# First-layer products of the coupling network made once, and its stages put in one rolling order over all cycles

## The reference

```python
def _twist(x):
    o_r, o_i, p_r, p_i = jnp.split(x, 4, axis=-1)
    return jnp.concatenate([p_r, -p_i, -o_r, o_i], axis=-1)
gf = _global_net(x.mean(axis=1, keepdims=True), ...)
out = x
for _ in range(NUM_CYCLES):                        # 3
    tf = _coupling_net(out, ...)   # gelu(h @ w1 + b1), 256 to 256; gelu to 128; gelu to 64; sigmoid to 1
    combined = 0.7 * gf + 0.3 * tf
    coupling = 0.1 + adaptive_range * (combined - 0.5) * 2.0
    out = out + coupling * _twist(out)
```

## Time and profile before

| what | value |
|---|---|
| median of 3 runs | 1000.38 us (997.75 to 1003.14) |
| profiled execution, its own time | 1000.18 us |
| its span in the trace | 998.4 us |
| PE busy | 925.4 us, 93% |
| DVE, ACT, POOL busy | 563.0, 473.3, 372.3 us |
| last piece of the attention's output product ends, coupling stages begin on PE | 886.28 us |
| last matmul | ends at 985.9 us |

### The profile page before, as it was taken

The page is one execution under the profiler, slowest core; times in us unless marked ns, Lnnn a source line. Parts: engine busy times, 40 slices in busy tenths (PEclk is TensorE's granted clock), DMA queues, the critical chain, the costliest instruction groups (busy, mean ns, idle before and its releaser), DMA issues.

```text
span 998.4 us, 20489 instructions
## 1 busy us (share of the span) xinstructions
PE 925.4 (93%) x6821; PEld 839.2 (84%) x6822; DVE 563.0 (56%) x1308; ACT 473.3 (47%) x1459; POOL 372.3 (37%) x498
## 2 busy tenths in 40 slices
PE   5999999999999897999999973899999999998994
PEld 3589999999999675999999973799999999985662
DVE  7564545555555483434433445777777776663273
ACT  0255555555555233443444452655555655534442
POOL 5153343343333203122222225756656543324132
PEclk9899999999999979999999995999999999999997
DMA  9400000020000065677777731200000000000002
GB/s 274 143 1 2 1 0 1 2 64 2 1 0 1 1 212 218 241 251 244 246 258 262 242 94 45 56 12 23 11 21 16 17 2 1 2 1 1 1 1 84
DMA packets 37503, 76.15 MB, mean 76 GB/s; under 512 B 5101, under 2 KB 23777, under 8 KB 37313
## 3 DMA queue, kind: packets, MB, share of 16 engines
q1 hardware_dynamic: 34033, 66.03, 20.0%
q0 software_dynamic: 3408, 9.31, 2.9%
HBM read 66.02 MB, written 9.31 MB: 75 GB/s over the span
## 4 chain that ended last, share of the span: by engine, by line
PE 85%; DVE 7%; POOL 2%; DMA 2%; ACT 2%; issue 2%; POOLq 0%; DVEq 0%; SPq 0%; ACTq 0%
PE banks L1527 14%; PE banks L470 11%; PE banks L472 11%; PE banks L471 11%; PE banks L504 9%; PE banks L478 7%; PE banks L489 6%; PE banks L496 3%; PE banks L619 3%; PE banks L1754 2%; PE banks L375 1%; PE banks L1758 1%; POOL W L1213 1%; DVE region_a L2060 1%; PE banks L1762 1%
## 5 line engine op out<-in xcount | busy, mean ns | idle before, releaser
L1527 PE MATMUL banks<-region_b,region_a 128*128 128x128 f32 x1248 | 145.9, 275 | 1.2 <-DMA region_a<-in_L_ffn_W 0.7
L1527 PEld LDWEIGHTS banks<-region_b,region_a 128*128 128x128 f32 x1248 | 142.8, 192 | 1.7 <-issue 0.9
L1090 ACT ACTIVATE region_a<-banks,negmax 128x154 f32<-128x154 f32 x256 | 96.0, 389 | 90.9 <-DVE negmax L833 89.6
L1243 POOL TENSOR_TENSOR region_a<-region_a,recip 128x512 f32<-128x512 f32 x64 | 66.5, 1040 | 178.6 <-DVE recip L839 178.6
L1278 POOL TENSOR_TENSOR region_a<-region_a,recip 128x640 f32<-128x640 f32 x64 | 80.2, 1253 | 104.0 <-DVE recip L965 103.7
L1617 DVE SCALAR_TENSOR_TENSOR region_b<-banks,region_a,region_b 128x128 f32<-128x128 f32 x156 | 43.9, 344 | 109.7 <-PE banks L1527 109.0
L504 PE MATMUL banks<-region_a 128*128 128x128 f32 x768 | 96.6, 276 | 1.9 <-DVE oT_low L856 1.8
L504 PEld LDWEIGHTS banks<-region_a 128*128 128x128 f32 x768 | 91.0, 192 | 2.9 <-issue 2.2
L478 PE MATMUL banks<-region_a 128*128 128x308 f32 x256 | 77.1, 424 | 0.0
L470 PE MATMUL banks<-Wo_high,oT_high 128*128 128x256 f32 x256 | 75.8, 296 | 0.9 <-DVE oT_low L856 0.9
L1152 ACT CAST pT_high<-banks 128x640 fp32r<-128x640 f32 x64 | 44.4, 694 | 66.3 <-PE banks L619 66.3
(11 more groups left out here) (248 smaller groups left out, 2454.0 us busy)
## 6 DMA issues: line engine op xcount, KB each, us to landing
region_a<-in_L_ffn_W SPq DMA_DIRECT2D x39, 1024.0 KB, 4.9
y_slots<-region_b SPq DMA_DIRECT2D x39, 128.0 KB
W<-in_L_ffn_W SPq DMA_DIRECT2D x1, 4096.0 KB, 17.3
xn_rows<-region_b SPq DMA_DIRECT2D x1, 2048.0 KB, 8.4
out<-x SPq DMA_DIRECT2D x4, 512.0 KB, 2.9
x<-in_x SPq DMA_DIRECT2D x1, 1536.0 KB, 13.0
region_b<-in_L_xattn_Wq SPq DMA_DIRECT2D x1, 1024.0 KB, 11.3
region_b<-in_L_xattn_Wo SPq DMA_DIRECT2D x1, 1024.0 KB, 13.9
```

The costliest lines, as they stand in the source:

```text
L1090: e = act.activation(pr[:, j, 0:L.keys], scores[:, g % 2, u, i * L.keys:(i + 1) * L.keys], ACT.Exp, bias=negmax[:, g % 2, j:j + 1], accum_ ...
L1243: pool.tensor_tensor(whole, pr[:, :, 0:split], rc.broadcast_to([P, L.hs, split]), ALU.mult)
L1527: mm = pe.matmul(banks[:, 2 * r + part, m * P:(m + 1) * P], W1[r][:, k, cols], xgT[:, r, k, :], start=(k == 0), stop=(k == DK - 1))
```

## The change

The twist J is linear, and J applied twice gives minus the input. So `out` after any number of cycles is a·x + b·J(x) for each token, with two numbers a and b of the token, and the first layer's product is a·(x W1) + b·(J(x) W1). The new kernel makes both products of the normalised rows once: a stage `uv_j.t` for each tile t of block j, with the turned rows as weights and [W1, J-turned W1] as 512 moving columns, so tokens are on partitions. ACT copies the left 256 columns to `U` (L1869 of the new kernel), DVE the right 256 to `JU` (L1982). `up_j.c` then transposes the block's combined rows back (8 transposes, L1800) straight into the bank from which ACT takes gelu; turn, `curT_high` and `curT_low` stay for cycle 0 alone. Between cycles DVE makes `mix` (4 instructions per block) and, once per block, `spin`. At the end `two_cycles` and `finish` form the gains from the coefficients of three cycles, ACT makes x = gain·cur + mean (`straight`, L1904), and DVE adds the gain times `turned_x` (L2044), which POOL makes once. Stores are of two tiles instead of four. All stages of all cycles stand in one list for PE and ACT (`PLAN`) and one for DVE (`MIXES`), with block numbers before the point and tile or cycle numbers behind it; `turn_2` is put between the two last output products.

```diff
-        EARLY = [("turn", 0), ("turn", 1)]
-        FIRST_ORDER = [("turn", 2), ("l1", 0), ("turn", 3), ("l1", 1)] + \
...
+        PLAN = plan("""uv_0.0 uv_0.1 uv_0.2 uv_0.3 turn_3 uv_1.0 up_0.0 uv_1.1 all_0 uv_1.2 all_1 l2_0.0 all_2 uv_1.3 l3_0.0
+                       uv_2.0 up_1.0 l4_0.0 uv_2.1 uv_2.2 l2_1.0 uv_2.3 l3_1.0
+                       uv_3.0 up_2.0 l4_1.0 uv_3.1 uv_3.2 l2_2.0 uv_3.3 l3_2.0
+                       up_3.0 up_0.1 l4_2.0 l2_3.0 l2_0.1 up_1.1 l3_3.0 l3_0.1 l2_1.1 l4_3.0 l4_0.1 up_2.1 l3_1.1
+                       l2_2.1 up_3.1 l4_1.1 l3_2.1 up_0.2 l2_3.1 l2_0.2 l4_2.1 l3_3.1 up_1.2 l3_0.2 l2_1.2 l4_3.1
+                       l4_0.2 up_2.2 end_0 l3_1.2 l2_2.2 l4_1.2 up_3.2 end_1 l3_2.2 l2_3.2 l4_2.2 end_2 l3_3.2 l4_3.2 end_3""")
+        MIXES = plan("""low_2 sum_2 first_2 even_0.0 even_0.1 even_0.2 even_0.3 low_3 sum_3 mean_0 even_1.0 even_1.1 even_1.2 even_1.3
+                        level_0 even_2.0 mix_0.0 even_2.1 even_2.2 spin_0 even_2.3 even_3.0 mix_1.0 even_3.1 even_3.2 spin_1
+                        even_3.3 mix_2.0 spin_2 mix_3.0 mix_0.1 spin_3 mix_1.1 mix_2.1 mix_3.1 gain_0 end_0 end_1 end_2 end_3""")
...
+        def pe_uv(pe, j, t):
+            n = 4 * j + t
+            pe.wait_ge(sem("turn_sb"), 2 * j + 1)
+            if j < 2:
+                pe.wait_ge(sem("turn_sb"), 2 * (2 * j + t // 2 + 1))
+            else:
+                pe.wait_ge(sem("u_sb"), n - 3)
+                pe.wait_ge(sem("ju_sb"), n - 3)
+            rows = slice(t * P, (t + 1) * P)
+            for k in range(DK):
+                mm = pe_split(pe, banks[:, uv_bank(j, t), :], (curT_high[:, j, k, rows], curT_low[:, j, k, rows]),
+                              (cw_high[:, k, :], cw_low[:, k, :]), k == 0, k == DK - 1)
...
+            def mixed(j, c):
+                coefficients(j, c)
...
+                for n in range(4 * j, 4 * j + 4):
+                    m = dve.scalar_tensor_tensor(block_rows(c + 1)[:, n, :], JU[:, n, :], c_up[:, c, n:n + 1],
+                                                 block_rows(c)[:, n, :], ALU.mult, ALU.add)
+                m.then_inc(sem("mix_ready"), 1)
...
+            def straight(j):
+                act.wait_ge(sem("gains_ready"), j + 1)
+                for n in range(4 * j, 4 * j + 4):
+                    act.activation(x[:, n, :], cur[:, n, :], ACT.Identity, bias=mean_var[:, n, 0:1],
+                                   scale=last_gains[:, n, 0:1]).then_inc(sem("x_straight"), 1)
...
+            for part in (cw_high, cw_low):
+                for k in range(DK):
+                    t = pool.tensor_tensor(part[:, k, D:2 * D], part[:, 1 - k, 0:D].bitcast(F32),
+                                           signs[:, 4 + k:5 + k].broadcast_to([P, D]), ALU.mult)
```

More of the change, by code:

```diff
@@ L1716, in cycles, with plan @@
[L1716 to L1720, removed]
+        def plan(text):
+            stages = []
+            for word in text.split():
+                kind, numbers = word.split("_")
+                stages.append((kind,) + tuple(int(n) for n in numbers.split(".")))
+            return stages
+        PLAN = plan("""uv_0.0 uv_0.1 uv_0.2 uv_0.3 turn_3 uv_1.0 up_0.0 uv_1.1 all_0 uv_1.2 all_1 l2_0.0 all_2 uv_1.3 l3_0.0
[4 more added lines that the diff above has]
+                       l4_0.2 up_2.2 end_0 l3_1.2 l2_2.2 l4_1.2 up_3.2 end_1 l3_2.2 l2_3.2 l4_2.2 end_2 l3_3.2 l4_3.2 end_3""")
@@ new lines, in pe_coupling @@
+            pe.wait_ge(sem("coupling_in"), 16 * LOADS)
+            pe.wait_ge(sem("cw_split"), 3)
+            for kind, *at_ in PLAN:
+                if kind == "turn":
+                    pe_turn(pe, *at_)
+                elif kind == "uv":
+                    pe_uv(pe, *at_)
+                elif kind == "all":
+                    pe_all(pe, *at_)
+                elif kind == "up":
+                    pe_up(pe, *at_)
+                elif kind == "l2":
+                    pe_l2(pe, *at_)
+                elif kind == "l3":
+                    pe_l3(pe, *at_)
+                elif kind == "l4":
+                    pe_l4(pe, *at_)
@@ new lines, in dve_coupling @@
+            for kind, *at_ in MIXES:
+                if kind == "low":
+                    turned_low(dve, *at_)
+                elif kind == "sum":
+                    turned_sum(dve, *at_)
+                elif kind == "first":
+                    last_cur()
+                elif kind == "even":
+                    even(*at_)
+                elif kind == "mean":
+                    mean()
+                elif kind == "level":
+                    levels()
+                elif kind == "mix":
+                    mixed(*at_)
+                elif kind == "spin":
+                    spin(*at_)
+                elif kind == "gain":
+                    two_cycles()
+                elif kind == "end":
+                    finish(*at_)
@@ new lines, in pool_coupling @@
+        def pool_coupling(pool):
+            pool.wait_ge(sem("o2_ps"), GROUPS)
+            for j in range(NB):
+                tiles = slice(4 * j, 4 * j + 4)
+                pool.wait_ge(sem("cur_first"), 4 * j + 4)
+                for h in range(2):
+                    src = slice(128, 256) if h == 0 else slice(0, 128)
+                    half = pool.tensor_tensor(
+                        turned_x[:, tiles, h * 128:(h + 1) * 128].rearrange("p t (s n) -> p t s n", s=2),
+                        cur[:, tiles, src].rearrange("p t (s n) -> p t s n", s=2),
+                        signs[:, 2 * h:2 * h + 2].unsqueeze(1).broadcast_to([P, 4, 2]).unsqueeze(3)
+                        .broadcast_to([P, 4, 2, 64]), ALU.mult)
+                half.then_inc(sem("x_turned"), 1)
@@ L2022, in _ @@
             pool.memset(V, 0.0).then_inc(sem("kv_zero"), 1)
+            pool.memset(signs[:, 0:4:3], 1.0)
+            pool.memset(signs[:, 1:3], -1.0)
+            for k, base, up in ((0, 64, 1), (1, -63, -1)):
+                pool.affine_select(out=signs[:, 4 + k:5 + k], in_=ones[:, 0:1], compare_op=ALU.is_ge, fill=-1.0, base=-base,
+                                   pattern=[[0, 1]], channel_multiplier=up)
             pool.memset(probs, 0.0).then_inc(sem("pads_zero"), 1)
```

431 lines of the change are left out of this document (236 added, 195 removed).

## The result

The new kernel takes 988.54 us (median of 4, 987.32 to 993.4) against 1000.36 us (997.75 to 1003.14) on the same chip, a ratio of 0.989, 95% interval 0.985 to 0.993. A second set of runs gave 988.08 and 0.987 (0.983 to 0.991). The forecast was 987.4, said as 987. The profiled execution takes 987.32 us, with a span of 985.5.

The account below looks back on a forecast made before the run. PE was taken to bound the stage up to 985.9, a chain without PE the end. PE 7.8 us less, tail 5.2 less, start 0.2 more took 1000.18 to 987.4 us; 8 in 10 within 979.5 to 995.5.

Parts of the forecast that it names:

- its work falls by 5.6 us: PE from 886.28 on: removed and added work alone, 87.3 us before against 81.7 after, gives 5.6 us.
- the carried 2.2: PE's time left unexplained in the earlier trace, put on first matmuls behind a change of operands: 2.2 us.
- the 81.7 of after: PE's summed work in the new kernel from 886.28, ending at 968.0 if it never waited.
- The seams' waits and slow stretches go: Between cycles: rows are ready 2.7 us behind l4, so PE's waits and both slow-clock stretches vanish.
- The middle, 1.0: Between the cycles' stages: gelus a few tenths late, as before l2_2.1 and l2_1.2, cost PE 1.0 us.
- The handover, 2.0: From attention to the coupling: first_cur and the reciprocal wait out POOL's turned_x, delaying turn_3 and the mean; 2.0 us.
- The tail, 6.1 and 1.0 for the clock: Last cycle: straight on ACT stands ahead of gelus PE needs, 6.1 us of waits, plus 1.0 for half clock.
- The rival half clock through the whole tail: Behind l4_0.2, 11.1 us of PE work at the low level costs 9.3 more: 995 us; chance 0.06.
- Behind the last l4, 7.3: After PE's end: tanh 0.45, gains 0.65, straight and DVE 2.2, store 4.0; 7.3 us, saving 5.2.
- DVE is no bound: Whole coupling: DVE has some 50 us of work against 80, so it does not bound.
- Cost at nothing: POOL's larger weight split, ending at 883.3 ahead of uv_0.0 at 887.15, and turned_x, needed 60 us later: no cost.
- The start, 0.2: Opening path: four signs instructions before POOL's last large memset delay the start by 0 to 0.5, taken as 0.2 us.

Follow-up runs that it names:

- e5: New kernel with the product of high rows by low weights left out of uv (32 of 96 matmuls); 985.46 us, 0.983 of the kernel before.
- e4: New kernel with PE's and ACT's stages in the order of one cycle after another; 987.10 us, 0.987 of the kernel before.
- e10: New kernel with straight on DVE and the stages in the order of one cycle after another; 987.86 us, 0.986 of the kernel before.
- e7: Kernel before, products still made in every cycle, with only the stages rolling over the seam and DVE's updates reordered; 999.64 us, 0.998 of the kernel before.
- e8: New kernel with two unread matmuls of l2's shape in PE's wait before the last l4; 985.66 us, 0.985 of the kernel before.
- e9: New kernel run again with no edit; 988.08 us, 0.987 of the kernel before.

## Why the prediction was right, point by point

- *PE bounds the stage until 960, and its work falls by 5.6 us.* The end came where it was forecast: PE was to end 978.1 - 886.28 = 91.8 us after the instant that lies one turn, 0.87 us, ahead of the first `uv`; it ended 979.31 - (887.86 - 0.87) = 92.3 after. The 5.6 is a slip of mine. The 87.3 of before lacks the carried 2.2 that the 81.7 of after contains; the terms say 87.3 + 2.2 - 81.7 = 7.8. The traces say about 5.7: without idle time and slow clock, before 99.6 - 6.5 - 3.6 = 89.5, after 92.3 - 6.1 - 2.4 = 83.8 (an estimate; the 6.1 is PE's idle time in the four windows up to 979.31). So 81.7 was 2.1 too short. An up takes up to 1.03 to the start of the next stage (959.76 to 960.79), where I had put 0.87, and an l2 1.91 (955.98 to 957.89), where I had put 1.72. e5 confirms the price of 0.233 behind `all_0`; ahead of it DVE sets the time.
- *The seams' waits and slow stretches go.* Held: 0.4 us idle in each window up to 955, and a clock of 1.00. The two went for different reasons. The waits for DVE went with the short chain: e4, in cycle order, has none. The slow stretch went only with both: it is there in e4 and e10, which lack the rolling order, and in e7, which has it alone and wins 2.7 us. The way from l4 to the next cycle's rows is short now, DVE alone, where before it was DVE, POOL, DVE. Its length was priced right: a mix takes 13.4 / 8 = 1.67 us (L2003 below).
- *The middle, 1.0.* Measured 0.7: waits of 0.35 us before l2_2.1 and l2_1.2, the two that were named. A third, before l2_2.2, belongs to the tail.
- *The handover, 2.0.* Mis-sized; it was 0.28 + 0.24. The waits are those before turn_3 and `all_0`. The DVE rows show first_cur at 1.68 for the pair, 0.95 longer than in the earlier trace rows, and the reciprocal at 0.24, not held at all, while POOL's `turned_x` ran. One instruction met POOL, not three, and uv_0 hid most of it. I had priced each as L1888's longest.

```profile
892.01 1.68 DVE L1927 TENSOR_SCALAR W<-x,mean_var,rstd 128x256 f32<-128x256 f32 x2
...
893.61 0.24 DVE L1960 RECIPROCAL W<-rstd 128x16 f32<-128x16 f32 x1
...
981.11 1.86 DVE L2044 SCALAR_TENSOR_TENSOR x<-W,x 128x256 f32<-128x256 f32 x4 [0.77 <-ACT x L1904]
...
890.45 8.13 POOL L2093 TENSOR_TENSOR W<-W,signs 128x512 f32<-128x512 f32 x8
```

- *The tail, 6.1 and 1.0 for the clock.* The mechanism held, and its sizes shifted: waits of 1.60, 0.35, 0.26 and 2.76 are 5.0 us, and the low clock costs 0.9 on the up, 0.7 on l3 and 0.8 on l4, 2.4 together. l4_1.2 started 6.0 us after l4_0.2, against 5.7 worked out. `straight` takes 2.07 per block, not 1.5: ACT's 128 x 256 out of SBUF with two operands per row is 0.59 in the groups below, where I had taken the 0.37 of a copy. That the last wait is 2.76 where 2.7 was worked out is luck: `straight` is 0.57 longer, and the gelu with its handover took 977.45 - 976.82 = 0.63, not 1.1. The rival half clock through the whole tail did not come; l2 and the l4 in between ran at the full rate.

```profile
L1904 ACT ACTIVATE x<-W,mean_var 128x256 f32<-128x256 f32 x16 | 8.3, 590 | 2.5 <-DVE W L2038 2.5
...
L2003 DVE SCALAR_TENSOR_TENSOR region_a<-region_b,W,region_a 128x256 f32<-128x256 f32 x32 | 13.4, 481 | 0.3
...
L1982 DVE COPY region_b<-banks 128x256 f32<-128x256 f32 x16 | 6.3, 415 | 12.5 <-ACT region_a L1869 12.5
```

- *Behind the last l4, 7.3.* It was 6.2. tanh, gains and the last products took 982.97 - 979.31 = 3.7, near the 3.3; behind the last DVE instruction lie 2.5 us instead of 4.0. The stores of 256 KB land in 2.1 us where 512 KB took 2.9. Of the 4.7 before, 998.4 - (993.7 + 2.9) = 1.8 lie behind the landing of the last store, of the 2.5 now 985.5 - (983.0 + 2.1) = 0.4. This difference I have not explained.
- *DVE is no bound.* Held: over the four windows above it is busy 50.6 us in sum, PE 87.3.
- *Cost at nothing.* The weight split on POOL ended at 883.55, ahead of its use at 887.86.
- *The start, 0.2.* POOL's second mean and rstd begin 0.36 us later, in line with the 0 to 0.5 given. How much of it reaches the end can't be read from single executions.

```profile
30.59 0.23 POOL L780 TENSOR_TENSOR mean_var<-mean_var,zero_eps 128x24 f32<-128x24 f32 x1 [10.52 <-DVE mean_var L771]
...
30.95 0.23 POOL L794 TENSOR_TENSOR mean_var<-mean_var,zero_eps 128x24 f32<-128x24 f32 x1 [11.40 <-DVE mean_var L785]
```

So the mechanisms were right in the main, and the closeness of the sum is in part luck. Against the forecast the handover was 1.5 us cheaper, the middle 0.3, the tail's waits 1.1 and the end behind the last l4 1.1; the low clock cost 1.4 more and PE's work 2.1 more.

The Trainium skill (Advanced Engine Details and Errata, VectorE Performance Modes) says that GPSIMD and two-port Vector instructions block each other. The trace agrees in kind, with first_cur held and the copies out of PSUM at 0.42 not, but the loss was 0.95 us for three such instructions in a row beside POOL, not one POOL instruction each.

What stays open: why the clock falls at one place of the tail in one execution and at another in the next.

## What to carry to other kernels

A rearranged order and a shortened chain both removed the waits at the seam: two of 2.33 us before, three of 0.37 in e7, none for DVE in e4. What the whole gains is another matter. Reordering alone gave 2.7 us, because the low clock stayed. The new form in the old order gave 12.3, but 5.1 of it lie behind the last l4 and by my estimate 5.7 are work that PE no longer does; waits for ACT and the low clock took back most of what the seams gave. The rolling order then looked worth 1.3 us, because waits in the tail hid what it saves; with `straight` on DVE it was 3.0 ahead of the last l4. So price a change again when another wait has gone. An engine with idle time still delays its neighbour when a long instruction stands ahead of a short one in its fixed order; look for who releases the wait, then for what that engine did just before. Price an instruction by a row of its own kind, operands and source included.

## What the runs showed of the hardware

The granted clock fell to the lower level without any wait of PE at the end of l3, l4, l3 and two l4 in a row, between 950 and 952 in e4, and at the end of the same five stages, between 952 and 954, in e10. In e7 it fell at 924 with one wait of 0.37 us ahead. Until then I had tied the fall to waits over 2 us; what else it hangs on is not shown. Filling a 2.8 us wait with two idle products kept the clock up behind it (e8), which is shown for this one place. Slow work ahead of a wait for another engine cost nothing (e9), behind it 0.9 us (new).

Beside POOL's instructions a pair of `first_cur` on DVE took 1.68 us instead of 0.73, and the addition to `cur` (128 x 1024, both inputs in SBUF) 2.06 instead of 1.23 in e7.
